# Pre-norm channel attention on one core: four last passes reordered per pair, two value passes moved to VectorE, last stores split

## The reference, cut to what matters

```python
def _gn(v, G=32, eps=1e-05):                      # group norm, 32 groups of 6 channels, no scale or shift
    g = v.reshape(B_, G, C_ // G, H_, W_)
    return ((g - mean(g)) / sqrt(var(g) + eps)).reshape(v.shape)

# x: (16, 192, 48, 48) float32; 8 heads of 24 channels; n = 2304 positions
xt = _gn(x).reshape(b, c, n).transpose(0, 2, 1)
q, k, v = split(xt @ w_qkv)                       # w_qkv: (192, 576)
q = q / norm over n;  k = k / norm over n;  k = k * temperature
attn = softmax(einsum('bhpn,bhnq->bhpq', k, q))   # 24 x 24 per head
out = einsum('bhnp,bhpq->bhnq', v, attn) @ w_out + b_out
return x + out.transpose back to (b, c, H, W)
```

## Time and profile before

| what | us |
|---|---|
| median of 3 runs | 352.33 (351.12 to 352.65) |
| the profiled execution's own time | 350.15 |
| its span | 348.4 |
| TensorE busy (matmuls) | 310.9 (89%) |
| VectorE busy | 284.4 (82%) |
| ScalarE busy | 242.9 (70%) |
| GpSimd busy | 145.8 (42%) |

### The profile page before, as it was taken

The page is one execution under the profiler, slowest core; times in us unless marked ns, Lnnn a source line. Parts: engine busy times, 40 slices in busy tenths (PEclk is TensorE's granted clock), DMA queues, the critical chain, the costliest instruction groups (busy, mean ns, idle before and its releaser), DMA issues.

```text
span 348.4 us, 9368 instructions
## 1 busy us (share of the span) xinstructions
PE 310.9 (89%) x3692; PEld 221.8 (64%) x3692; DVE 284.4 (82%) x705; ACT 242.9 (70%) x447; POOL 145.8 (42%) x129
## 2 busy tenths in 40 slices
PE   0039858999999999999999999999999999999895
PEld 0027736765678667866787567866787568856552
DVE  5999894896999689986998699968998685278874
ACT  1089689867997599759996699759986899640300
POOL 0059679303870178315750287115930586002000
PEclk9999987999999999999999999999999999999999
DMA  7999920004995279915994399627992574016876
GB/s 225 355 322 259 246 77 2 3 1 144 301 350 164 92 208 349 301 52 169 305 310 127 119 292 328 216 93 186 320 322 63 154 235 132 3 48 181 283 215 229
DMA packets 30828, 67.75 MB, mean 194 GB/s; under 512 B 5504, under 2 KB 12096, under 8 KB 30784
## 3 DMA queue, kind: packets, MB, share of 16 engines
q1 hardware_dynamic: 30544, 66.56, 61.3%
q10 hardware_dynamic: 240, 0.59, 0.6%
HBM read 29.38 MB, written 28.31 MB: 166 GB/s over the span
## 4 chain that ended last, share of the span: by engine, by line
PE 72%; ACT 8%; issue 7%; DVE 6%; SPq 2%; DMA 2%; POOL 2%; ACTq 0%; POOLq 0%; DVEq 0%
PE u_ps L1015 29%; PE g_ps L1015 20%; PE s_ps L1015 10%; PE u_ps L1066 4%; PE u_ps L1067 4%; ACT tok L613 3%; ACT h_sb L575 2%; DMA wo<-in_L_conv_w_out_dram 2%; PE u_ps L1068 2%; PE u_ps L1069 2%; ACT xn L566 2%; DVE x_sb L938 1%; SPq L381 1%; POOL l_sb L503 1%; SPq L386 1%
## 5 line engine op out<-in xcount | busy, mean ns | idle before, releaser
L503 POOL TENSOR_TENSOR l_sb<-xn,h_sb 128x768 f16<-128x768 f32 x63 | 103.2, 1652 | 49.3 <-ACT h_sb L575 49.3
L938 DVE SCALAR_TENSOR_TENSOR x_sb<-u_ps,bias,x_sb 128x384 f32<-128x384 f32 x144 | 83.7, 610 | 13.6 <-PE u_ps L1015 13.0
L1015 PE MATMUL g_ps<-tok 128*128 128x64 f16 (+1 forms) x864 | 86.4, 240 | 4.1 <-ACT tok L613 4.0
L613 ACT COPY tok<-u_ps 128x384 f32<-128x384 f32 x144 | 65.7, 484 | 17.3 <-PE u_ps L1069 16.0
L799 DVE BATCH_NORM_STATS2 bnst<-x_sb 128x6 f32<-128x384 f32 x144 | 71.5, 545 | 4.0 <-DMA x_sb<-in_x_dram 3.9
L1015 PEld LDWEIGHTS g_ps<-tok 128*128 128x128 f16 x864 | 57.2, 99 | 27.5 <-ACT tok L613 6.5
L1015 PE MATMUL u_ps<-h_sb,ml 128*128 128x384 f16 (+1 forms) x336 | 72.7, 326 | 0.0
L566 ACT ACTIVATE xn<-x_sb,rb 128x768 f32<-128x768 f32 x60 | 59.6, 1026 | 14.0 <-POOL rb L515 14.0
L575 ACT ACTIVATE h_sb<-x_sb,rb 128x768 f16<-128x768 f32 x63 | 64.3, 1034 | 0.4 <-POOL rb L515 0.4
L1066 PE MATMUL u_ps<-id,h_sb 128*128 128x128 f16 x288 | 49.2, 224 | 6.1 <-DVE l_sb L779 5.3
L1067 PE MATMUL u_ps<-id,l_sb 128*128 128x128 f16 x288 | 49.2, 224 | 0.0
(11 more groups left out here) (149 smaller groups left out, 527.0 us busy)
## 6 DMA issues: line engine op xcount, KB each, us to landing
x_sb<-in_x_dram SPq DMA_DIRECT2D x48, 384.0 KB, 5.5
out_dram<-x_sb SPq DMA_DIRECT2D x48, 384.0 KB, 3.5
out_dram<-x_sb SPq DMA_DIRECT2D x48, 192.0 KB, 3.2
x_sb<-in_x_dram SPq DMA_DIRECT2D x45, 192.0 KB, 5.0
hl<-h_sb SPq DMA_DIRECT2D x48, 96.0 KB, 3.2
hl<-l_sb SPq DMA_DIRECT2D x48, 96.0 KB, 3.4
x_sb<-in_x_dram ACTq DMA_DIRECT2D x3, 192.0 KB, 4.2
w<-in_L_conv_w_qkv_dram SPq DMA_DIRECT2D x1, 288.0 KB, 7.2
```

Source lines behind the costliest of these rows:

```text
L503: nc.gpsimd.tensor_tensor(l_sb[:, par, t, cols], xn[:, c % XN_RING, :], h_sb[:, par, t, cols], ALU.subtract).then_inc(l_ok, 1)
L613: nc.scalar.copy(tok[:, j % TOK_RING, :, :].rearrange("p b n -> p (b n)").bitcast(F32), slot_words(j)).then_inc(tok_a, 1)
L938: V.scalar_tensor_tensor(out=xs, in0=block_ps(n), scalar=bias[:, t:t + 1], in1=xs, op0=ALU.add, op1=ALU.add).then_inc(out_ok, 1)
L1015: return nc.tensor.matmul(dst, lhs, rhs, start=start, stop=stop, skip_group_check=True)
```

## The change

Five edits. In stage A of the steady steps ScalarE runs "exp" and then "h7" after copy 5 (before: "h7" after copy 4, "exp" after copy 5), and "h8" after copy 8 instead of copy 7. In the head's second step VectorE makes the values of chunks 6 and 7 ("v6" in its stage B of the first step, "v7" behind "soft_in"), ScalarE's x6 and x7 are gone and its h5, h6, h7 lie after copies 0, 1, 2, x8 after copy 4, "exp" and h8 after copy 5; "flip" moves from slot 3 to 1, "v" from 10 to 9, "m" from 13 to 12. `channel_stats` takes the three parts as the upper 16 bits of float32 words, which leaves out two conversions (`STAT` 6 to 4). GpSimd's waits on the values follow who makes them. The last chunk's stores are cut into halves of 384 columns, image one from SyncE's queue and image two from ScalarE's.

```diff
-ACT_A = {1: ["h6"], 3: ["x8"], 4: ["h7"], 5: ["exp"], 7: ["h8"], 11: ["v"], 14: ["m"]}
+ACT_A = {1: ["h6"], 3: ["x8"], 5: ["exp", "h7"], 8: ["h8"], 11: ["v"], 14: ["m"]}
...
-               1: ["t1", "lo", "bn", "norms", "wo", "spread", "bn", "bn", "bn"]}
+               1: ["t1", "lo", "bn", "norms", "wo", "spread", "bn", "v6", "bn", "bn"]}
...
-BY_VECTOR_1 = 3
-SECOND_PE_A = {3: ["flip"], 10: ["v"], 13: ["m"]}
-SECOND_ACT_A = {0: ["h5"], 1: ["x6"], 2: ["h6"], 3: ["x7"], 4: ["h7"], 5: ["x8"], 6: ["exp"], 7: ["h8"], 12: ["v"], 15: ["m"]}
+BY_VECTOR_1 = (0, 1, 2, 6, 7)
+SECOND_PE_A = {1: ["flip"], 9: ["v"], 12: ["m"]}
+SECOND_ACT_A = {0: ["h5"], 1: ["h6"], 2: ["h7"], 4: ["x8"], 5: ["exp", "h8"], 12: ["v"], 15: ["m"]}
+SECOND_VEC_A = {**VEC_A, 0: ["soft_in", "v7"]}
...
-        mv = sb("mv", [P, 3, 2])
+        moments = sb("moments", [P, 3, 3, 2])
+        mv = moments[:, 0, :, :]
-        parts = sb("parts", [P, 3, 3, 2], BF16)
+        parts = moments[:, :, :, :].rearrange("p a t s -> p (a t s)").bitcast(BF16).rearrange(
+            "p (a t s h) -> p a t s h", a=3, t=3, s=2)[:, :, :, :, 1]
...
-        STAT, GVAR, NORM, SOFT, ATTN = 6, 4, 2, 5, 6
+        STAT, GVAR, NORM, SOFT, ATTN = 4, 4, 2, 5, 6
...
+                        if p == PAIRS - 1 and k == NC_ - 1:
+                            for i in (0, 1):
+                                sp.wait_ge(out_ok, done[k] - 1 + i)
+                                chip, dram = ends([c + i * BW for c in at[g]], image, o_d, t, g * GW + i * BW, BW)[0]
+                                sp.dma_start(dram, chip).then_inc(stored[t][g], 16)
...
-                    if q == 1 and c < BY_VECTOR_1:
-                        pool.wait_ge(xn1_vec, c + 1)
+                    if q == 1 and c in BY_VECTOR_1:
+                        pool.wait_ge(xn1_vec, BY_VECTOR_1.index(c) + 1)
...
+            def last_store():
+                t, g = ROWS[-1]
+                q = PAIRS - 1
+                for i in (0, 1):
+                    c = g * GW + i * BW
+                    act.wait_ge(out_ok, (q + 1) * NO + NO - 1 + i)
+                    act.dma_start(o_d[2 * q + 1:2 * q + 2, P:C, c:c + BW].rearrange("o c n -> (o c) n"),
+                                  xcol(q, t, c, BW)[C1:P, :]).then_inc(stored[t][g], 16)
...
+                need(dve, l_ok, c + 1 - XN_RING)
...
-                ch.then(V.tensor_copy(parts[:, 0, :, :], mv[:, :, :]))
-                ch.then(V.tensor_tensor(res1[:, :, :], mv[:, :, :], parts[:, 0, :, :], ALU.subtract))
-                ch.then(V.tensor_copy(parts[:, 1, :, :], res1[:, :, :]))
-                ch.then(V.tensor_tensor(parts[:, 2, :, :], res1[:, :, :], parts[:, 1, :, :], ALU.subtract))
+                for k in (0, 1):
+                    ch.then(V.tensor_tensor(moments[:, k + 1, :, :], moments[:, k, :, :], parts[:, k, :, :], ALU.subtract))
```

More of the change, by code:

```diff
@@ L174, in preact_attention @@
         bnst = sb("bnst", [P, 3, NB * 6])
-        mv = sb("mv", [P, 3, 2])
+        moments = sb("moments", [P, 3, 3, 2])
+        mv = moments[:, 0, :, :]
         msq = sb("msq", [P, 3])
-        parts = sb("parts", [P, 3, 3, 2], BF16)
-        res1 = sb("res1", [P, 3, 2])
-        res2 = sb("res2", [P, 3, 2])
+        parts = moments[:, :, :, :].rearrange("p a t s -> p (a t s)").bitcast(BF16).rearrange(
+            "p (a t s h) -> p a t s h", a=3, t=3, s=2)[:, :, :, :, 1]
         gsum = sb("gsum", [P, 3, 2])
@@ L404, in step @@
                         t, g = ROWS[k]
-                        sp.wait_ge(out_ok, done[k])
-                        for chip, dram in ends(at[g], image, o_d, t, g * GW, GW):
-                            sp.dma_start(dram, chip).then_inc(stored[t][g], 16)
+                        if p == PAIRS - 1 and k == NC_ - 1:
[3 more added lines that the diff above has]
+                                sp.dma_start(dram, chip).then_inc(stored[t][g], 16)
+                        else:
+                            sp.wait_ge(out_ok, done[k])
+                            for chip, dram in ends(at[g], image, o_d, t, g * GW, GW):
+                                sp.dma_start(dram, chip).then_inc(stored[t][g], 16)
                     if more and k >= LOAD_LAG:
@@ L455, in _ @@
             for t, g in ROWS:
-                sp.wait_ge(stored[t][g], PAIRS * (32 if t == 1 else 16))
+                sp.wait_ge(stored[t][g], PAIRS * (32 if t == 1 else 16) + (32 if (t, g) == ROWS[-1] else 0))
         @block.gpsimd
@@ L498, in split @@
                     pool.wait_ge(h_ok, (q - 1) * NC_ + c + 1)
-                    if q == 1 and c < BY_VECTOR_1:
-                        pool.wait_ge(xn1_vec, c + 1)
-                    else:
-                        pool.wait_ge(xn_ok, (q - 1) * NC_ + c + 1 - BY_VECTOR_1)
+                    if q == 1 and c in BY_VECTOR_1:
+                        pool.wait_ge(xn1_vec, BY_VECTOR_1.index(c) + 1)
+                    else:
+                        by_vector = len(BY_VECTOR_1) if q > 1 else sum(k < c for k in BY_VECTOR_1)
+                        pool.wait_ge(xn_ok, (q - 1) * NC_ + c + 1 - by_vector)
                     nc.gpsimd.tensor_tensor(l_sb[:, par, t, cols], xn[:, c % XN_RING, :], h_sb[:, par, t, cols],
@@ L711, in step @@
                         small_steps[what](p + 1)
+            def last_store():
[6 more added lines that the diff above has]
+                                  xcol(q, t, c, BW)[C1:P, :]).then_inc(stored[t][g], 16)
             for_pairs(act, step)
+            last_store()
         @block.vector
@@ L788, in second_value @@
                     dve.wait_ge(low_ok, 4)
-                V.tensor_scalar(xn[:, c, :], xcol(1, t, g * GW, GW), rb[:, 1, 0, t:t + 1], rb[:, 1, 1, t:t + 1],
+                need(dve, l_ok, c + 1 - XN_RING)
+                V.tensor_scalar(xn[:, c % XN_RING, :], xcol(1, t, g * GW, GW), rb[:, 1, 0, t:t + 1], rb[:, 1, 1, t:t + 1],
                                 ALU.mult, ALU.add).then_inc(xn1_vec, 1)
@@ L979, in step @@
                 for j in range(SLOTS):
-                    for what in hooks(p, FIRST_VEC_A, VEC_A, LAST_VEC_A, PAIRS - 1).get(j, ()):
+                    for what in hooks(p, FIRST_VEC_A, VEC_A, LAST_VEC_A, PAIRS - 1, SECOND_VEC_A).get(j, ()):
                         if what == "stats":
@@ L985, in step @@
                             pieces(now, 1)
+                        elif what == "v7":
+                            second_value(7)
                         elif small:
@@ L1002, in step @@
                             mixed_weights()
-                        elif what in ("v0", "v1", "v2"):
+                        elif what in ("v0", "v1", "v2", "v6"):
                             second_value(int(what[1]))
```

## The result

| | kernel before | changed kernel |
|---|---|---|
| runs beside the first measurement | 351.73 us median of 4 (350.56 to 352.65) | 346.85 us median of 4 (346.41 to 347.9) |
| all runs of this study | 350.78 us median of 77 (349.44 to 353.88) | 346.76 us median of 10 (346.41 to 348.76) |
| profiled execution, its span | 350.15, 348.4 | 347.9, 346.1 |

The first measurement gives a ratio of 0.9867 (95% interval 0.9827 to 0.9908). The same kernel run again beside 29 runs of the kernel before gives 0.9882 (0.9852 to 0.9911). The change is faster by 1.2 to 1.3%: 4.7 us by the first ratio (3.2 to 6.1), 4.1 by the second (3.1 to 5.2), 4.0 by the medians of all runs, against the 3.0 forecast. The forecast was 349.3, with 347.3 as the low end of the range, and 346.85 lies under it.

A forecast was written before the change was run, and what follows sets the result against it. The prediction took TensorE's waits, and what lies before its first and behind its last matmul, as the bound. 0.6 + 1.3 + 0.3 + 0.8 = 3.0 us off 352.33 gave 349.3 us, range 347.3 to 351.1.

The forecast's parts named there:

- The sum, 3.0: Whole kernel: gains of steady pairs 0.6, head 1.3, statistics 0.3 and end 0.8 add up to 3.0 us.
- Steady pairs, 0.6: Stage A, six steady pairs: TensorE's wait moves from gram pass 5 to 6, shrinking 0.41 to 0.30; 0.6 us.
- Head, 1.3: Head's second step: fewer ScalarE passes and earlier flip, v, m cut TensorE's waits; 1.3 us, bounds 0.3 to 1.6.
- The value pass beside GpSimd: Head: v6 held up by GpSimd's low half 4, ending 0.44 after that half's normal end, at 58.36.
- Statistics, 0.3: Sums of a pair with late loads: two conversions fewer remove TensorE's wait of 0.31; 0.3 us, between 0 and 0.7.
- End, 0.8: Last stores: halves on two queues issue 0.5 sooner and land sooner; 0.8 us, between 0.3 and 1.1.
- Rival 4: End: two queues save the issue only, 0.5 there, 2.7 us in all, 349.6 us; chance 0.2.
- Rival 1: Steady pairs: pass 6 waits as long as pass 5 did; gain 1.6 in all, 350.7 us; chance 0.13.
- Rival 2: Head: v6 and v7 both block at 1.73 on the shared port; gain 2.0 in all, 350.3 us; chance 0.1.
- Rival 3: Steady pairs: low half 8 too late for transposes behind gram pass 9; 4.8 us slower, 357.1 us; chance 0.03.

The follow-up runs named there:

- 9: Kernel before with half the stores of the first seven pairs left out and the shorter statistics chain: 350.37 us, ratio 0.9972.
- 6: Kernel before with ScalarE's new steady table alone (exp, then h7 after copy 5, h8 after copy 8): 349.49 us, ratio 0.9975.
- 7: Kernel before with the head's edit alone (values of chunks 6 and 7 by VectorE, flip, v and m sooner): 349.42 us, ratio 0.9950.
- Experiment 10: Changed kernel with h7 one copy later in the steady pairs, after copy 6: 346.35 us, ratio 0.9856.
- experiment 5: Changed kernel again, unchanged, beside many more runs of the kernel before: 346.66 us, ratio 0.9882.
- experiment 1: Kernel before with the shorter statistics chain alone: 350.09 us, ratio 0.9977.

## Why the prediction was right or wrong

- **Where it ended.** Faster by over 0.5% was right. The step that failed is the last, "The median of the runs, 352.33, lies 2.2 above that execution; the terms don't depend on it, so I forecast 352.33 - 3.0". Three runs of a kernel that scatters from 349.4 to 353.9 are a poor base: 77 runs have their median at 350.78, 1.55 lower. Of the 2.45 between forecast and result 1.55 is the base, 1.0 the sum (3.0 where 4.0 was measured), and 0.1 the other way the draw of the four runs. The range was laid around the wrong base and missed by 0.45; reaching 5 below 351.73, the base measured beside the result, it would just have held it.
- **Luck.** The profiled execution less the sum, 347.15, came within 0.3 of the result and 0.4 of the median of all ten runs. It is no better a base: that one execution lay 0.6 below its kernel's median, and the sum was 1.0 too small, so two errors nearly cancelled.
- **The sum, 3.0.** It measured 4.0 to 4.1 in the larger sets of runs. No place of waiting was missed; the steady pairs were 0.3 to 0.5 short, the head 0.2 by the stages, and what the statistics are worth stays open between a few tenths and the timed 0.8.
- **Steady pairs, 0.6.** The wait moved to pass 6 as forecast, but at 0.24 instead of 0.30. I took 0.06, 0.16 and 0.93 for the latency, the exponential and h7; they were 0.04, 0.15 and 0.91, and the rest of the 0.06 is hundredths. Over six pairs that is 0.4 us, and I had rounded 0.66 down to 0.6. The gain is 1.1 by the stages, 0.9 by the ratio (6, interval 0.1 to 1.6).
- **Head, 1.3.** Each step stands in the trace: v6 1.31 (1.35 worked out), v7 0.67, pass 16 without its wait. Without the 0.25 by which the whole head lay later, the exponential came at 61.48 (61.66 worked out) and pass 9 at 65.40 (65.62): softmax_in began 0.1 sooner behind v6, and from its first step to the exponential it took 2.30 instead of 2.38. So the gain is 1.51 by the stages; 1.8 by the ratio (7, interval 0.8 to 2.7). One addition of the prediction is off: 62.1 + 2 x 1.65 is 65.4, not 65.5. It changes nothing, and low half 8 ended at 65.42 without the 0.25.
- **The value pass beside GpSimd.** v6 began while GpSimd was in a low half (56.52 to 58.17 by its usual 1.65) and ended at 58.58, 0.41 behind it; the pass beside the low half took 1.31 and the free one 0.67. The row of before, 0.44 behind the low half, gave 58.6 with the head's 0.25. The Trainium skill (SBUF — State Buffer, "Who interferes with whom") says that the later one fully blocks. The trace agrees as to who waits; the literal reading, a full 0.67 after the low half, would be 58.84, so the row was the better guide.
- **Statistics, 0.3.** The traces bear the mechanism out: in a late pair the sums come at most 2.30 after the first output block with the short chain, 2.4 to 2.7 with the old one in the worst pairs (9). But the wait of 0.31 was not the price of the late pair: its stage B was 0.67 longer than the others, and with the short chain 0.4 of such a stage stays. The timed gains of 0.8 and 1.1 have intervals that reach down to nothing, so they neither confirm nor refute the 0.3. I sized it from one execution with one late pair; how many a run has on average isn't known.
- **End, 0.8.** 0.80 in the traces; 0.7 by the ratio, which can't tell 0.5 or even nothing from 0.8 (interval -0.1 to 1.4). Rival 4 wanted 0.5. The traces show more than the issue: the last issue starts 0.5 sooner after the result, and the slower of the two queues lands its 96 KB in 2.4 where the slower of the last 192 KB stores took 2.7. Whether fewer bytes or the second queue makes it sooner isn't separated. By the Trainium skill (DMA: Bandwidth & Descriptors, "Issuing engines are not separate DMA queues") a second issuer saves only the time of issuing; that part of the gain is the 0.5, and the other 0.3 came with stores of half the size.
- **The other rivals.** Rival 1: pass 6 waits 0.24, not 0.41, false. Rival 2: v7 wasn't blocked, false. Rival 3: low half 8 ended 0.44 ahead, false. Experiment 10 came closer to it: low half 8 ended no later, but TensorE was there sooner, and 0.17 was left.

## What to carry to other kernels

When a long pass between two short copies makes the consumer wait, place it where the copies have the most lead. A wait that only moved one slot on may be movable once more, as here from pass 6 away altogether; look first at what else then gets tight. Take the base of a forecast from many runs, not from three and not from one profiled execution: here the base was off by 1.55, more than any term of the sum. Where one queue both stores and loads, leave room between a store and the wait for its landing: one chunk less of it cost this kernel 6.6 us.

## What the runs showed of the hardware that I had not expected

- The head's start scatters with the landing of the weights. ScalarE's first pass and gram pass 0, in the trace of experiment 7 (the head alone) and of experiment 5 (the changed kernel again, an execution of 348.76):

```profile
16.84 0.52 ACT L592 ACTIVATE wh<-w 128x384 f16<-128x384 f32 x1 [12.61 <-DMA wo<-in_L_conv_w_out_dram]
```
```profile
18.36 0.52 ACT L599 ACTIVATE wh<-w 128x384 f16<-128x384 f32 x1 [14.13 <-DMA wo<-in_L_conv_w_out_dram]
```
```profile
26.88 1.06 PE L1037 MATMUL g_ps<-tok 128*128 128x384 f16 x6
```

  The same loads, issued in the same order and 0.3 us apart (that of `wo` at 9.30 and 9.62), landed 1.5 us apart, and all that follows moved with them (gram pass 0 at 25.35 in the first of the two). Part of the 1 to 4 us between a kernel's fastest and slowest run may be this and late loads; how much each, these traces don't say.
- Late loads fall on other pairs from execution to execution, with 0.15 to 2.2 us of idle time at one spot as long as the load order is the old one. More waiting doesn't mean a longer run in proportion: in the steady pairs of the changed kernel VectorE waited 5.2 us for loads and the stages lost about 1.5; in experiment 1 it waited 2.7 and no stage was longer by more than 0.05; in the kernel before it waited 1.1 and lost 0.7.
- However late a load was, it delayed the sums only so far. With the short chain, waits of 0.8 to 2.85 us at one spot all gave sums at most 2.30 after the first output block (2.08 is on time); the rest of the lateness went into stage A, where the first output block itself came up to 1.4 later.
